# An attention and mixture-of-experts kernel on one Trainium2 core: semaphores by kind of weight, additions spread over three tiles, four result buffers, and the second token tile loaded ahead of the context

## The reference

```
x = x + xattn(layernorm(x), ctx)     # 16 heads of 32, causal mask, first 112 rows of a context of 128 features
    q = x @ Wq.T;  k, v = split(ctx @ Wkv.T);  softmax(q k / sqrt(32)) v @ Wout.T
x = x + ffn(layernorm(x))
    scores  = softmax(x @ gate.T)                    # 8 experts, the 2 best of each token
    routed  = sum over 2 experts: weight * (silu(x @ G_e.T) * (x @ U_e.T)) @ D_e.T      # inner width 352
    shared  = (silu(x @ G.T) * (x @ U.T)) @ D.T      # inner width 704
    x + routed + shared
```

## Time and profile before

| | us |
|---|---|
| median of 3 runs | 351.81 (350.88 to 352.39) |
| profiled execution, its own time | 353.07 |
| its span, first to last instruction | 351.3 |
| TensorE busy in it | 332.9 |
| VectorE busy | 271.6 |
| ScalarE busy | 230.0 |
| GpSimd busy | 118.5 |

### The profile page before, as it was taken

One profiled execution on the slowest core, in us unless ns is written; L12 is line 12 of the kernel. 1 busy time (PEld: TensorE's weight loads), 2 busy tenths in 40 slices (PEclk: granted clock), 3 DMA queues, 4 the chain that ended last, 5 costly groups with the idle time before them and its releaser, 6 DMA issues.

```text
span 351.3 us, 7091 instructions
## 1 busy us (share of the span) xinstructions
PE 332.9 (95%) x2281; PEld 280.5 (80%) x2282; DVE 271.6 (77%) x464; ACT 230.0 (65%) x586; POOL 118.5 (34%) x136
## 2 busy tenths in 40 slices
PE   6999989999999999999999999999999999999980
PEld 6898877777776797988897878898889889988860
DVE  4798978999946258835586998999899899989900
ACT  3577899999973233213235578888888888888720
POOL 3332753555541000256200033343244234324411
PEclk9999999999999999999999999999999999999996
DMA  7999100000003799993599735434443543444233
GB/s 253 368 349 380 64 3 2 3 2 2 2 2 108 284 331 387 400 355 129 169 292 246 261 101 86 93 60 72 82 88 60 82 92 67 67 82 91 30 41 49
DMA packets 29051, 49.47 MB, mean 141 GB/s; under 512 B 7136, under 2 KB 12256, under 8 KB 28000
## 3 DMA queue, kind: packets, MB, share of 16 engines
q1 hardware_dynamic: 24880, 39.91, 35.0%
q0 software_dynamic: 4144, 9.23, 15.0%
HBM read 32.22 MB, written 16.92 MB: 140 GB/s over the span
## 4 chain that ended last, share of the span: by engine, by line
PE 54%; ACT 14%; DVE 10%; DMA 9%; issue 5%; POOL 4%; SPq 1%; POOLq 1%; ACTq 0%; DVEq 0%
PE bank L837 22%; PE bank L524 19%; ACT prob L956 8%; PE bank L854 5%; POOL xs_dram L474 4%; DMA xs_dram<-x2n,slot_i 3%; DMA w_dn<-dnT 3%; PE bank L708 2%; PE bank L876 2%; ACT probT L911 2%; PE bank L737 1%; DMA out<-y_sb,dest 1%; DVE xres L1391 1%; DMA w_sg<-sguT 1%; DMA ctx<-ctxT 1%
## 5 line engine op out<-in xcount | busy, mean ns | idle before, releaser
L1186 DVE TENSOR_TENSOR gu_parts<-w_gu,gu_parts 128x704 fp32r<-128x704 f32 x84 | 78.9, 972 | 1.7 <-ACT gu_parts L911 1.6
L911 ACT ACTIVATE gu_parts<-w_gu 128x704 fp32r x84 | 66.2, 794 | 18.4 <-PE bank L837 17.2
L837 PE MATMUL bank<-gu_parts,xsT_hi 128*128 128x352 f32 x336 | 69.5, 328 | 0.8 <-DVE xsT_lo L1186 0.8
L837 PEld LDWEIGHTS bank<-gu_parts,xsT_hi 128*128 128x128 f32 x336 | 55.6, 189 | 1.6 <-issue 1.2
L493 POOL CAST dn_hi<-w_dn 128x512 fp32r x20 | 19.7, 984 | 101.0 <-PE bank L524 69.0
L505 POOL DMA_INDIRECT out<-y_sb,dest x21 | 33.3, 1585 | 22.9 <-ACT y_sb L1116 17.2
L837 PE MATMUL bank<-gu_parts,xsT_lo 128*128 128x352 f32 x168 | 40.9, 325 | 0.0
L524 PE MATMUL bank<-x2T_hi,w_sg_lo 128*128 128x512 f32 (+1 forms) x88 | 32.6, 371 | 0.3
L524 PE MATMUL bank<-x2T_hi,w_sg_hi 128*128 128x512 f32 (+1 forms) x88 | 32.0, 363 | 0.0
L524 PE MATMUL bank<-x2T_lo,w_sg_hi 128*128 128x512 f32 (+1 forms) x88 | 31.9, 363 | 0.0
L837 PEld LDWEIGHTS bank<-gu_parts,xsT_lo 128*128 128x128 f32 x168 | 29.3, 189 | 0.0
(11 more groups left out here) (196 smaller groups left out, 804.9 us busy)
## 6 DMA issues: line engine op xcount, KB each, us to landing
w_gu<-guT SPq DMA_DIRECT2D x8, 1408.0 KB, 9.7
xs_dram<-no_row SPq DMA_DIRECT2D x1, 5460.0 KB, 19.2
xs_in<-xs_dram SPq DMA_DIRECT2D x21, 256.0 KB, 2.6
w_dn<-dnT SPq DMA_DIRECT2D x8, 512.0 KB, 6.2
w_sg<-sguT SPq DMA_DIRECT2D x10, 256.0 KB, 5.6
w_dn<-dnT SPq DMA_DIRECT2D x8, 192.0 KB, 6.7
w_sd<-sdnT SPq DMA_DIRECT2D x5, 256.0 KB, 4.8
out<-xres SPq DMA_DIRECT2D x1, 1280.0 KB, 5.4
```

The lines of the kernel that those rows point to most:

```text
L837: ins = pe.matmul(dst[:, 0:F], xsT[x_][:, c, :], gu2[w_][:, c, f0:f0 + F], start=c == 0 and n == 0, stop=c == C - 1 and n == 2)
L911: act.activation(dst, src, ACT.Copy).then_inc(s[sem], 1)
L1186: dve.tensor_tensor(lo_, src, hi_.bitcast(F32), ALU.subtract).then_inc(s[sem], 1)
```

## The change

- **Semaphores.** `we` is split into `wegu` (the eight gate-up loads) and `wedn` (the early down loads); `we_late` is now `wedn_late`. ScalarE waits only for `wegu` before it casts gate-up weights, and for the two others before its first cast of down weights. On GpSimd the first expert number is loaded ahead of the waits.
- **Additions.** The last slice's seven additions stood, one by one, behind the four remainders of tile 0's gate-up weights, two more behind these, and one behind tile 0. Now the first four stand ahead of each remainder, one more behind, one behind tile 1 and one behind tile 2. SyncE issues the second store accordingly after the loads of tiles 3 and 4.
- **Results.** `y_sb` has four buffers. On GpSimd, of tiles 0 to 3 each scatter stands behind the cast for the tile two on (one on before).
- **End.** The down product of tile 19 stands between the halves of the last gate-up, ScalarE scales that result before it takes the silu of tile 20, and there are 8 and 4 filling transposes in place of 5.
- **Start.** Token tile 1 is loaded ahead of the context, tiles 2 and 3 behind the first query weights; VectorE takes tile 1's statistics and applies tile 0's normalisation ahead of the context's remainder, tile 1's ahead of tile 0's transposed remainder; two casts (`ident_r`, `mask_r`) move behind the statistics of tile 5; tile 1 is transposed after two key products, not three; ScalarE casts the first query weights ahead of the first two copies of keys; six filling transposes go.

The diff, without renamings of `we` on SyncE:

```diff
@@ -162,6 +162,8 @@
     y_sb = [m.inside(loop, f"y_sb{i}", [P, H]) for i in range(2)]
+    y_sb += [nc.alloc_sbuf_tensor_at(f"y_sb{i + 2}", [P, H], F32, offset=act0_at + 4 * H * i) for i in range(2)]
+    NY = len(y_sb)
@@ -263,11 +265,12 @@
             sp.dma_start(xres[:, 0, :], x_rows[0:P, :]).then_inc(s["x0"], 16)
+            sp.dma_start(xres[:, 1, :], x_rows[P:2 * P, :]).then_inc(s["xt1"], 16)
             load_ctx(0)
             sp.dma_start(w_kv[:, 0:H], wkvT[:, 0:H]).then_inc(s["wkeys"], 16)
-            sp.dma_start(xres[:, 1, :], x_rows[P:2 * P, :]).then_inc(s["xt1"], 16)
-            sp.dma_start(xres[:, 2:BLK, :], tiles_of(x_rows, 2, BLK)).then_inc(s["xt2"], 16)
             for c in range(C):
+                if c == 1:
+                    sp.dma_start(xres[:, 2:BLK, :], tiles_of(x_rows, 2, BLK)).then_inc(s["xt2"], 16)
                 sp.dma_start(w_q[:, c, :], wqT[c * P:(c + 1) * P, :]).then_inc(s[f"wq{c}"], 16)
@@ -365,9 +368,12 @@
             load_x(2)
+            for i in (3, 4):
+                sp.wait_ge(s["Tx"], i)
+                load_x(i)
             sp.wait_ge(s["sres"], NX * ND)
             start_sum(BLK + 1, NX)
-            with sp.Fori(3, NT) as i:
+            with sp.Fori(5, NT) as i:
                 sp.wait_ge(s["Tx"], i)
@@ -482,20 +488,23 @@
             pool.wait_ge(s["pos"], 3)
-            pool.wait_ge(s["we"], 16 * (3 * E - 2 * n_late))
-            pool.wait_ge(s["we_late"], 16 * 2 * n_late)
-            pool.wait_ge(s["sdn"], NX * ND)
...
                 e = pool.value_load(eid[0:1, i:i + 1], min_val=0, max_val=E - 1)
-                if i >= 1:
+                if i == 0:
+                    pool.wait_ge(s["wedn"], 16 * 2 * (E - n_late))
+                    pool.wait_ge(s["wedn_late"], 16 * 2 * n_late)
+                    pool.wait_ge(s["sdn"], NX * ND)
+                else:
                     pool.wait_ge(s["edn_split"], i)
...
             dn_hi1(0)
+            dn_hi1(1)
             for i in range(NT):
-                if i + 1 < NT - 1:
-                    dn_hi1(i + 1)
+                ahead = 2 if i < NY else 1
+                if i != NY and i + ahead < NT - 1:
+                    dn_hi1(i + ahead)
                 if i == 0:
@@ -504,7 +513,7 @@
                     out=out[:, :], out_offset=bass.IndirectOffsetOnAxis(ap=dest[:, i, 0:1], axis=0),
-                    in_=y_sb[i % 2][:, :], in_offset=None, compute_op=ALU.add).then_inc(s["yst"], 16)
+                    in_=y_sb[i % NY][:, :], in_offset=None, compute_op=ALU.add).then_inc(s["yst"], 16)
@@ -613,10 +622,9 @@
             for j in range(C):
-                if j == C - 1:
+                if j == 2:
                     t1(1, S[1])
                 k_proj(0, j, bank[4 + j])
-            keep_busy(S[2:4], 3)
@@ -884,8 +892,8 @@
             pe.wait_ge(s["pos"], 3)
-            pe.wait_ge(s["we"], 16 * (3 * E - 2 * n_late))
-            pe.wait_ge(s["we_late"], 16 * 2 * n_late)
+            pe.wait_ge(s["wedn"], 16 * 2 * (E - n_late))
+            pe.wait_ge(s["wedn_late"], 16 * 2 * n_late)
             down(0, expert(0))
@@ -896,11 +904,13 @@
             e_last = [expert(i) for i in (NT - 2, NT - 1)]
-            gate_up(NT - 1)
+            gate_up(NT - 1, range(C // 2))
             pe.wait_ge(s["ey"], NT - 2)
             down(NT - 2, e_last[0])
+            gate_up(NT - 1, range(C // 2, C))
+            fill_with_transposes(S[2], 8)
             t_act(NT - 1)
-            fill_with_transposes(S[2], 5)
+            fill_with_transposes(S[2], 4)
             pe.wait_ge(s["sres"], NX * ND)
@@ -983,9 +993,9 @@
             put_xnT(0, S[0])
+            wq_hi(0)
             put_kT(0, 0, bank[4])
             put_kT(0, 1, bank[5])
-            wq_hi(0)
             put_xnT(1, S[1])
@@ -1111,16 +1121,16 @@
                 act.wait_ge(s["edn"], i + 1)
-                if i >= 2:
-                    act.wait_ge(s["yst"], 16 * (i - 1))
-                act.activation(y_sb[i % 2][:, :], A[:, :], ACT.Copy, scale=dest[:, i, 1:2].bitcast(F32))\
+                if i >= NY:
+                    act.wait_ge(s["yst"], 16 * (i - NY + 1))
+                act.activation(y_sb[i % NY][:, :], A[:, :], ACT.Copy, scale=dest[:, i, 1:2].bitcast(F32))\
                     .then_inc(s["ey"], 1)
             def put_last_y(i):
-                act.wait_ge(s["yst"], 16 * (i - 1))
+                act.wait_ge(s["yst"], 16 * (i - NY + 1))
                 for n, (bank_, at, width) in enumerate(last_parts):
                     act.wait_ge(s["edn"], i + 1 + n)
-                    ins = act.activation(y_sb[i % 2][:, at:at + width], bank_[:, 0:width], ACT.Copy,
+                    ins = act.activation(y_sb[i % NY][:, at:at + width], bank_[:, 0:width], ACT.Copy,
                                          scale=dest[:, i, 1:2].bitcast(F32))
@@ -1135,7 +1145,7 @@
             act.wait_ge(s["pos"], 3)
-            act.wait_ge(s["we"], 16 * (3 * E - 2 * n_late))
+            act.wait_ge(s["wegu"], 16 * E)
@@ -1148,16 +1158,17 @@
                 if i == NT - 1:
+                    put_y(i - 1)
                     silu(i)
                     put_last_actT(i)
-                    put_y(i - 1)
                     break
...
                     act.wait_ge(s["sdn"], NX * ND)
-                    act.wait_ge(s["we_late"], 16 * 2 * n_late)
+                    act.wait_ge(s["wedn"], 16 * 2 * (E - n_late))
+                    act.wait_ge(s["wedn_late"], 16 * 2 * n_late)
                     act.wait_ge(s["dest"], 16)
@@ -1268,11 +1279,10 @@
+            dve.wait_ge(s["xt1"], 16)
+            stats1(1)
+            apply1(0)
             ctx_lo(0)
-            dve.wait_ge(s["const"], 3)
-            dve.tensor_copy(ident_r[:, :], ident[0:SQ, 0:SQ]).then_inc(s["pmask"], 1)
-            dve.tensor_copy(mask_r[:, :, :], mask[:, :, :]).then_inc(s["pmask"], 1)
-            apply1(0)
@@ -1282,10 +1292,8 @@
             wkv_lo(0)
-            dve.wait_ge(s["xt1"], 16)
-            stats1(1)
+            apply1(1)
             xnT_lo(0, S[0])
-            apply1(1)
             wq_lo(0)
@@ -1302,6 +1310,9 @@
             stats1(5)
+            dve.wait_ge(s["const"], 3)
+            dve.tensor_copy(ident_r[:, :], ident[0:SQ, 0:SQ]).then_inc(s["pmask"], 1)
+            dve.tensor_copy(mask_r[:, :, :], mask[:, :, :]).then_inc(s["pmask"], 1)
             wkv_lo(1)
@@ -1505,9 +1516,9 @@
                     xs_lo(0)
+                add_shared(ND - 1, 0, c, c + 1)
                 gu_lo(e, 0, c)
-                add_shared(ND - 1, 0, c, c + 1)
-            add_shared(ND - 1, 1, 0, 2)
+            add_shared(ND - 1, 1, 0, 1)
             for i in range(NT):
@@ -1524,7 +1535,9 @@
                     dve.tensor_copy(act_last[0:w, 2, :], B[0:w, 2 * P:3 * P]).then_inc(s["aT_last"], 1)
-                if i == 0:
+                if i == 1:
+                    add_shared(ND - 1, 1, 1, 2)
+                if i == 2:
                     add_shared(ND - 1, 1, 2)
```

14 lines of the change are left out of this document (7 added, 7 removed).

## The result

| | median us (range, runs) | ratio to before, 95% interval |
|---|---|---|
| before | 351.90 (350.88 to 353.91, 9) | |
| changed | 356.10 (353.58 to 358.69, 9) | 1.0114 [1.0087, 1.0140] |

The change makes the kernel 1.1% slower, 4.0 us. I had predicted 350.7 us and given "slower" a chance of 0.05; the time is also above the range. The profiled execution of the changed kernel took 356.06 us (span 354.2, clock 0.994), 2.99 more than that of before. Its runs also spread wider.

A forecast was written before the change was run, and what follows sets the result against it. TensorE was taken to bound the kernel, so savings count only where it waits or the end hangs on another engine. Terms -0.6 - 0.8 - 1.0 + 2.5 - 1.2 = -1.1 gave 350.7 us; range 348.0 to 352.3.

The forecast's parts named there:

- Entry: Start of the expert stage: first gate-up no longer waits for an addition on VectorE; 0.8 us gained, bounds 0.3 and 0.9.
- Second wait: Gate-up of tile 2: no longer late for the remainder of its rows on VectorE; 1.0 us gained, bounds 0.4 and 1.1.
- The queue: GpSimd's casts and scatters in one order: late scatters delay casts; 2.5 us lost, bounds 0 and 4.0.
- S0: Start of the scatter of tile 0's result: predicted at 219.8, 11.5 us later than before.
- G8: Start of tile 8's gate-up: predicted near 249.6, unhindered 247.1, a loss of 2.5 us.
- S4: Start of the scatter of tile 4's result: predicted at 242.9, ahead of the cast for tile 6.
- Rival B: GpSimd's queue with landings of 5.4 throughout: 4.0 us lost, median 352.2; chance 0.1.
- Tail: End of the kernel: last two scatters issued earlier; 1.2 us gained, bounds 0.7 and 1.5.
- S19: Start of the scatter of tile 19's result: predicted at 337.2 to 337.7 instead of 339.24.
- S20: Start of the scatter of tile 20's result: predicted at 343.7 against 344.92, held by its own result.
- Start: Before the first scores: tile 1 ready sooner for the first query product; 0.6 us gained, bounds 0 and 1.1.
- Rival C: The start gains nothing, as the token load only changes places with the awaited load; median 351.3; chance 0.15.

The follow-up runs named there:

- a: The changed kernel with VectorE's spread additions and the second store put back where the kernel before has them; 352.12 us, ratio 1.0000.
- i: The kernel before with the new entry alone (split semaphores, number loaded ahead of GpSimd's waits, first additions ahead of weight remainders); 351.48 us, ratio 0.9980.
- g_again: The same kernel as g, run a second time beside after_again; 350.97 us, ratio 0.9956 to the kernel before.
- g: The changed kernel with additions and second store put back, and GpSimd casting one tile ahead throughout; 350.77 us, ratio 0.9969.
- h: The same kernel as g, but with the program's start put back as in the kernel before; 351.18 us, ratio 0.9970.
- after_again: The changed kernel itself, run once more; 356.93 us, ratio 1.0117 to the kernel before.
- b: The changed kernel with GpSimd casting two tiles ahead to the end, so that no two scatters stand in a row; 357.24 us, ratio 1.0148.
- u_unrolled: The changed kernel with TensorE's tile loop written out and each expert's number loaded a tile ahead; 355.56 us, ratio 1.0105.

## Why the prediction was wrong

By its own steps:

- **Entry, -0.8: right in size in the trace** (2.64 for 3.53), though part of it goes back to the row load of tile 1. I had read only what VectorE and ScalarE do there, not what had had slack. Before, that load was issued at 190.96, landed 5.8 later and was needed at 197.88, 1.1 us of slack; in the changed kernel it was issued at 191.16 and took 6.5, so that it landed near 197.7, while without the wait of 0.45 TensorE would have come to it at 197.27.
- **Second wait, -1.0: right in the changed kernel's profile if counted from G1** (1.07 at G2). With the additions back the step from G1 to G2 is 7.36 in three profiles (a, i, g_again) and 8.0 to 8.2 in two (g, h, with 0.75 and 0.70 of issue), against 7.89 before; in after_again it is 7.91, with 0.66 of issue. So spreading the additions shortens this step by 0.5. Counted from the first gate-up, though, G2 comes after 13.23 in the changed kernel and 13.27 in a and g_again, against 13.91 before: the row load takes the 0.5 again, and the 0.6 to 0.7 that do reach G2 are there without the spread additions. These cost 4.0 behind.
- **The queue, +2.5: this step failed.** The mechanism was right to the place: S0 predicted for 219.8 and found at 220.12, the loss at G5 and G8, VectorE idle for GpSimd's cast. The size was not, by a factor of two: 5.2 in the profile, 5.1 to 5.5 by the runs. The terms: S0 followed G3 after 6.61, not 6.9 (-0.3); S4 followed S0 after 24.16, not 23.1 (+1.1), since landings were 5.53, 4.68, 5.33 and 5.61 where I had taken 5.4 and three times 4.9; G8 followed S4 after 7.87, not 6.67 (+1.2; the parts that I named for it sum to 6.6); and G9 lost another 0.8, which I had at nothing. Together 2.5 + 2.7.
- Two of these could have been priced from the rows of before. The median of all landings was the wrong one: 4.9 is that of steady tiles, and the earlier trace rows had 5.4 for the one scatter that started late. Most of the difference is the issue itself, which a landing time includes: GpSimd was held 1.57 us by a steady scatter (landing 3.3 after that), 1.94 by S0 of before (3.5), and 2.32, 1.59, 2.15 and 2.03 by the four of the chain (3.2, 3.1, 3.2 and 3.6). In b the scatters of tiles 6 to 17 come 0.16 behind a cast each; their issue takes 2.03 and the landing 5.2 to 5.5. What lengthens the issue in the chain isn't shown.
- The other is the time from VectorE's remainder of the rows to the gate-up: at the second wait 207.15 to 207.91. I named that 0.76 for G2 and left it out for G8, where it was 1.09 (251.06 to 252.15). It isn't there at every gate-up: in u_unrolled, with TensorE's loop written out, it is 0.10, G8 follows S4 after 6.90, near my 6.67, and G9 loses nothing. In that trace these two terms go away with the head of the loop; by the runs this is open.
- **Rival B had the mechanism and too small a price**: landings of 5.4 throughout were its case, 4.0 its loss and 0.1 its chance. The landings measured 5.3 on the mean, and the loss was larger still.
- **Tail, -1.2: 0.83 in this pair of traces**, 0.4 to 0.9 over all of them, 0.5 by the runs. S19 came 6.2 after G20, as predicted; S20, which hangs on the last result as I had it, came 12.8 after it and not 12.4.
- **Start, -0.6: 0.** The 0.4 at the first scores in one profile is within what profiles differ by. Rival C was right about it. The granted clock did not fall at the start without the filling transposes, as I had read. It did fall behind stalls of the expert stage, in four of the profiles made later, which I had not considered.

The parts as measured (start 0, entry -0.7, tail -0.5, queue +5.1 to +5.5) sum to 3.9 to 4.3; the change costs 4.0. As the queue is taken from the distance between the changed kernel and g, what this tests is the rest: the parts give -1.2, and g has -1.1 and -1.5.

## What to carry to other kernels

Where casts and transfers share an engine's queue, and each transfer waits for the one before, moving the first transfer later is paid wherever the next engine needs a cast until the queue has caught up. More buffers for the data did not prevent it here, since the order is what waits. Price such a chain with the landings of transfers that start as it does, not with the median over the program, and count from the last landing to the product that starts, with every gap that the nearest row shows. When a wait is removed, list the loads whose slack it was.
